# Mixture of experts after an RWKV block on one core: blocks of first choices before blocks of second choices, and one row of results per token

## The reference

```python
x = x + _layernorm(rwkv(_layernorm(x)))    # k, v, r products, a scan over time, output product
x = x + _layernorm(ffn(_layernorm(x)))

# ffn, with E = 8 experts, K = 2 choices, F = 256
probs = softmax(xf @ router_w)
topw, topi = top_k(probs, 2)
routed = sum over the two choices of topw * (silu(xf @ w1[e]) @ w2[e])
shared = silu(gate) * up @ shared_down     # gate, up = halves of xf @ shared_gate_up
shared = sigmoid(xf @ shared_gate_w) * shared
return routed + shared
```

## Time and profile before

| | us |
|---|---|
| median of 3 runs | 1823.32 (1821.41 to 1824.04) |
| the profiled execution | 1822.15 |
| its span, first to last instruction | 1820.0 |
| stage 1, until the first block is loaded | to 1128.82 |
| stage 2, until the results' first load | 1128.82 to 1656.10 |
| stage 3 | 1656.10 to 1820.0 |
| granted TensorE clock, mean | 0.927 of full speed |

### The profile page before, as it was taken

The page is one execution under the profiler, slowest core; times in us unless marked ns, Lnnn a source line. Parts: engine busy times, 40 slices in busy tenths (PEclk is TensorE's granted clock), DMA queues, the critical chain, the costliest instruction groups (busy, mean ns, idle before and its releaser), DMA issues.

```text
span 1820.0 us, 34848 instructions
## 1 busy us (share of the span) xinstructions
PE 1514.6 (83%) x9764; PEld 1345.2 (74%) x9764; DVE 1469.1 (81%) x3533; ACT 1393.5 (77%) x2577; POOL 1074.7 (59%) x985
## 2 busy tenths in 40 slices
PE   4899999999999999999999835999999999980000
PEld 3678888888888888888888734999888888870000
DVE  4799989999998989989898754887776777764888
ACT  3799999999999999999999863776666666651444
POOL 1245545455564645556464441688888888886556
PEclk8999999999999999999999966999999999995555
DMA  5123434343332433333342234898888888877997
GB/s 202 47 89 115 139 116 133 118 148 102 118 128 97 142 106 128 109 116 122 106 142 84 93 108 151 243 189 148 145 145 145 144 144 145 147 114 230 415 417 305
DMA packets 184044, 274.67 MB, mean 151 GB/s; under 512 B 17713, under 2 KB 139569, under 8 KB 183857
## 3 DMA queue, kind: packets, MB, share of 16 engines
q1 hardware_dynamic: 132688, 201.37, 32.6%
q0 software_dynamic: 51168, 71.07, 22.1%
HBM read 127.53 MB, written 144.85 MB: 150 GB/s over the span
## 4 chain that ended last, share of the span: by engine, by line
PE 54%; issue 11%; POOL 11%; DMA 8%; DVE 7%; ACT 3%; DVEq 1%; SPq 1%; ACTq 0%; POOLq 0%
PE PS L1289 42%; POOL d_y L547 8%; PE PS L1281 3%; PE PS L1465 3%; PE PS L1483 2%; POOL d_xd L522 2%; DMA d_y<-x,ixb 2%; PE PS L1352 1%; DMA al<-d_y 1%; DMA shh<-d_y 1%; DMA d_y<-nx,ixb 1%; PE PS L1350 1%; DVE bst L881 1%; PE PS L1443 1%; DVEq L1244 1%
## 5 line engine op out<-in xcount | busy, mean ns | idle before, releaser
L522 POOL DMA_INDIRECT d_xd<-h2n,ixs x256 | 321.2, 1255 | 275.1 <-DVE h2n L1060 194.4
L1289 PE MATMUL PS<-hTh,wqh 128*128 128x512 f32 x768 | 306.5, 399 | 15.8 <-ACT kk L581 10.5
L1289 PE MATMUL PS<-hTh,wql 128*128 128x512 f32 x768 | 306.6, 399 | 0.0
L1289 PE MATMUL PS<-hTl,wqh 128*128 128x512 f32 x768 | 306.2, 399 | 0.0
L1289 PEld LDWEIGHTS PS<-hTh,wqh 128*128 128x128 f32 x768 | 146.4, 191 | 50.7 <-ACT kk L581 11.4
L547 POOL DMA_INDIRECT d_y<-xin,ixb x90 | 141.7, 1575 | 52.6 <-DVE xin L1235 27.0
L1289 PEld LDWEIGHTS PS<-hTh,wql 128*128 128x128 f32 x768 | 146.2, 190 | 34.6
L1289 PEld LDWEIGHTS PS<-hTl,wqh 128*128 128x128 f32 x768 | 146.1, 190 | 33.6
L547 POOL DMA_INDIRECT d_y<-x,ixb x90 | 142.3, 1581 | 27.4 <-issue 20.7
L547 POOL DMA_INDIRECT d_y<-nx,ixb x90 | 141.5, 1572 | 27.4 <-issue 22.6
L482 POOL TENSOR_SCALAR var<-mv 128x4 f32<-128x4 f32 x64 | 62.5, 977 | 148.9 <-DVE mv L886 148.7
(11 more groups left out here) (301 smaller groups left out, 5630.5 us busy)
## 6 DMA issues: line engine op xcount, KB each, us to landing
d_y<-ysh SPq DMA_DIRECT2D x64, 512.0 KB
xin<-in_L_attn_x SPq DMA_DIRECT2D x32, 512.0 KB, 3.9
x<-in_L_attn_x SPq DMA_DIRECT2D x32, 512.0 KB, 3.9
d_x<-x SPq DMA_DIRECT2D x32, 512.0 KB
kk<-d_xd SPq DMA_DIRECT2D x34, 272.0 KB
vv<-d_xd SPq DMA_DIRECT2D x34, 272.0 KB
tr<-d_xd SPq DMA_DIRECT2D x34, 272.0 KB
dl<-d_xd SPq DMA_DIRECT2D x33, 272.0 KB
```

The costliest lines, as they stand in the source:

```text
L522: g.indirect_dma_start(d_xd, bass.IndirectOffsetOnAxis(ap=ixs[:, k:k + 1], axis=0), h2n[:, j, :], None).then_inc(s_sct, 16)
L1289: ins = mm_(out_ap, l, r, start=(k == 0), stop=(k == len(todo) - 1))
```

## The change

- `d_xd` becomes two tensors, one for first choices and one for second. Ranks, positions, counts and tables have a leading axis of 2. Stage 2 has two halves of NB1 = 71 blocks each (64 + 7), NB = 142 in all.
- The shared expert's row is no longer written to `d_y` by SP (64 stores of 512 KB). POOL scatters it (`shared_scatter`, 4 indirect DMAs a chunk) to `d_xs`, at the row that the token's first choice has in its block. In the first half of stage 2 SP loads 256 rows of `d_xs` into `yb` beside each block (`load_shared`), `y_out` adds the expert's result to them, and POOL scatters the sum to `d_y` without adding in DRAM. In the second half the scatter adds in DRAM as before. Between the halves POOL waits for all of its scatters of the first.
- `d_y` has one row per token. Stage 3 loads 512 KB a chunk instead of twice that, and `total` is gone. 14 chunks of x1 instead of 12 are loaded during stage 2.
- The zero blocks: SP writes 8 + 3 before stage 2, ACT writes 8 (for `d_xs`) behind its last `shared_out`, and SP the 8 for second choices between the first loads of stage 2.
- Banks and order in stage 1: `pV[1]` and `pU[0]` move to PS0, `pRK` to PS4; the second `gate_up_product` of `pU` moves ahead of `proj(0, i-1, 0)`; `weighed` moves behind `shared` on DVE; `own_exp` moves to the end of the step before on ACT. `shared_out` of a chunk waits until the rows of the chunk before have been scattered.

```diff
-    NB = 2 * N // BLK + E - 1
+    NF = N // BLK
+    NB1 = NF + E - 1
+    NB = 2 * NB1
...
-        pV = [PS[1], PS[5]]
+        pV = [PS[1], PS[0]]
...
-        pU = [PS[4], PS[3]]
+        pU = [PS[0], PS[3]]
...
-        pRT, pRK = PS[0], PS[0]
+        pRT, pRK = PS[0], PS[4]
...
# SP, stage 1
-                if on(i - 6):
-                    sp.wait_ge(s_ys, n(i - 6, NT, NT))
-                    for s in range(2):
-                        sp.dma_start(ys_a[s, i - 6], ysh[:, :, :]).then_inc(s_st2, 16)
...
+            def tail_2(e):
+                r = sp.value_load(tail[0:1, 1, e:e + 1], min_val=0, max_val=E * CAP - BLK)
+                sp.dma_start(d_xd[1][bass.ds(r, BLK), :].rearrange("(p j) d -> p j d", p=P), zt).then_inc(s_tail2, 16)
...
# SP, before stage 2
+            sp.wait_ge(s_tail, 16 * (2 * E + 3))
+            sp.wait_ge(s_scy, 16 * NT * NCH)
...
+            def load_shared(b):
+                if b >= NYB:
+                    sp.wait_ge(s_yo[b % NYB], 32 * (b // NYB))
+                r = sp.value_load(tabx[0:1, 0, b:b + 1], min_val=0, max_val=E * CAP)
+                sp.dma_start(yb[b % NYB], d_xs[bass.ds(r, BLK), :].rearrange("(p j) d -> p j d", p=P)
+                             ).then_inc(s_yl[b % NYB], 16)
...
             for b in range(NB):
+                if b == NB1:
+                    sp.wait_ge(s_tail2, 16 * E)
                 load_block(b)
+                if 1 <= b <= E:
+                    tail_2(b - 1)
...
+                if 0 <= b - 2 < NB1:
+                    load_shared(b - 2)
                 if b >= 8 and b - 8 < NS:
                     load_rest(b - 8)
...
# POOL
+            def shared_scatter(m):
+                pool.wait_ge(s_pl, n(m, NPL, L_IX))
+                for j in range(NT):
+                    pool.wait_ge(s_ys, n(m, NT, j + 1))
+                    g.indirect_dma_start(d_xs, bass.IndirectOffsetOnAxis(ap=ixs[:, m % 2, j:j + 1], axis=0),
+                                         ysh[:, j, :], None).then_inc(s_scy, 16)
...
-            for i in range(NCH + 4):
+            for i in range(NCH + 6):
...
+                if on(i - 4):
+                    scale_o(i - 4)
+                if on(i - 5):
+                    scatter(i - 5, 0)
+                    scatter(i - 5, 1)
+                if on(i - 4):
+                    scale_h2(i - 4)
                 if 0 < i < NCH:
                     scale_in(i)
+                if on(i - 6):
+                    shared_scatter(i - 6)
...
+                if w < NB1:
+                    for j in range(2):
+                        g.indirect_dma_start(d_y, bass.IndirectOffsetOnAxis(ap=ixb[:, w % 8, j:j + 1], axis=0),
+                                             yb[w % NYB][:, j, :], None).then_inc(s_yo[w % NYB], 16)
+                else:
+                    if w == NB1:
+
+                        for i in range(NYB):
+                            pool.wait_ge(s_yo[i], 32 * ((NB1 - i + NYB - 1) // NYB))
...
# ACT
-                    act.wait_ge(s_st2, 32 * m)
+                    act.wait_ge(s_scy, 16 * NT * m)
...
+            act.wait_ge(s_zt, 2)
+            act.wait_ge(s_tab, 1)
+            for e in range(E):
+                r = act.value_load(tail[0:1, 0, e:e + 1], min_val=0, max_val=E * CAP - BLK)
+                A.dma_start(d_xs[bass.ds(r, BLK), :].rearrange("(p j) d -> p j d", p=P), zt[:, :, 0:D]).then_inc(s_tail, 16)
             A.preload_act_table(ACT.Silu)
...
# DVE, stage 1
-                if on(i - 3):
-                    weighed(i - 3)
                 if on(i - 5):
                     shared(i - 5)
                 if on(i - 3):
+                    weighed(i - 3)
                     sums(i - 3)
...
# DVE, stage 2
+                    if w < NB1:
+                        V.scalar_tensor_tensor(out=t, in0=part, scalar=cwb[:, w % 8, j:j + 1], in1=t, op0=ALU.mult,
+                                               op1=ALU.add).then_inc(s_y, 1)
+                    else:
+                        V.tensor_scalar(t, part, cwb[:, w % 8, j:j + 1], None, ALU.mult).then_inc(s_y, 1)
...
# DVE, stage 3
-                V.tensor_tensor(oC[c % NO], y0C[c % NY], y1C[c % NY], ALU.add).then_inc(s_sum, 1)
...
# PE, stage 1
-                    free((i - 4, s_pl, NPL, L_TB), (i - 4, s_ro, NRO, R_LG), (i - 2, s_k, 2, 2))
+                    free((i - 4, s_mul, 2, 1), (i - 4, s_ro, NRO, R_LG), (i - 2, s_v, 2, 2), (i - 2, s_k, 2, 2))
                     proj(0, i - 1, 1, pK, s_pk)
```

More of the change, by code:

```diff
@@ L52, in rwkv_moe @@
     out_c = out.rearrange("b (c p j) d -> (b c) p (j d)", j=NT, p=P)
-    d_xd = nc.dram_tensor("d_xd", [E * CAP + BLK, XW], F32).ap()
-    NSINK = E + NB - NF + 1
-    d_y = nc.dram_tensor("d_y", [2 * N + 1 + NSINK * BLK, D], F32).ap()
-    ys_a = d_y[1:2 * N + 1, :].rearrange("(s c j p) d -> s c p j d", s=2, j=NT, p=P)
+    d_xd = [nc.dram_tensor(f"d_xd{s}", [E * CAP + BLK, XW], F32).ap() for s in range(2)]
+    d_xs = nc.dram_tensor("d_xs", [E * CAP + BLK, D], F32).ap()
+    NSINK = E + NB1 - NF + 1
+    d_y = nc.dram_tensor("d_y", [N + 1 + NSINK * BLK, D], F32).ap()
     with ExitStack() as ctx:
@@ L275, in rwkv_moe @@
         s_yo = [sem(f"s_yo{i}") for i in range(6)]
+        s_yl = [sem(f"s_yl{i}") for i in range(6)]
         s_Tx = sem("s_Tx")
@@ L286, in rwkv_moe @@
         s_y = sem("s_y")
-        s_cx = [sem(f"s_cx{i}") for i in range(12)]
-        s_cy2 = [sem(f"s_cy2{i}") for i in range(6)]
-        s_sum = sem("s_sum")
+        s_cx = [sem(f"s_cx{i}") for i in range(14)]
         s_nrm = sem("s_nrm")
@@ L386, in _ @@
             sp.dma_start(x1[:, :, :], x_v[0]).then_inc(s_xr, 16)
-            for i in range(NCH + 6):
+            for i in range(NCH + 4):
                 if i % 2 == 0 and i // 2 < E:
@@ L475, in _ @@
             for e in range(E):
-                last = g.memset(tb[:, e:e + 1], float(e * CAP))
+                last = g.memset(tb[:, :, e:e + 1], float(e * CAP))
             last.then_inc(s_const, 1)
@@ L762, in _ @@
             for i in range(NCH + 5):
-                if on(i - 3):
-                    own_exp(i - 3)
                 if on(i - 5):
@@ L807, in _ @@
                     alpha(i - 2)
+                    own_exp(i - 2)
                 if on(i - 3):
@@ L837, in _ @@
                 act.wait_ge(s_nb[3 + c % 2], c // 2 + 1)
-                act.wait_ge(s_sum, c + 1)
+                if c >= NO:
+                    act.wait_ge(s_out[c % NO], 16 * (c // NO))
                 for j in range(NT):
                     at = slice(j * D, (j + 1) * D)
-                    A.activation(oC[c % NO][:, at], oC[c % NO][:, at], ACT.Identity, scale=rstd[:, 3 + c % 2, j:j + 1],
+                    A.activation(oC[c % NO][:, at], yC[c % NY][:, at], ACT.Identity, scale=rstd[:, 3 + c % 2, j:j + 1],
                                  bias=nb[:, 3 + c % 2, j:j + 1]).then_inc(s_nrm, 1)
@@ L1193, in _ @@
             step(4)
-            V.tensor_tensor_scan(cum[:, :], ones8[:, :], nbk[:, :], zero[:, 0:1], ALU.mult, ALU.add).then_inc(s_tb, 1)
-            V.tensor_scalar(wstep[:, :], nbk[:, :], -float(BLK), float(CAP), ALU.mult, ALU.add).then_inc(s_tb, 1)
-            step(6)
-            V.tensor_tensor(big[:, :, :], iotb[:, :].unsqueeze(2).to_broadcast([P, NBP, E]),
-                            cum[:, :].unsqueeze(1).to_broadcast([P, NBP, E]), ALU.is_ge).then_inc(s_tb, 1)
+            for s in range(2):
+                V.tensor_tensor_scan(cum[:, s, :], ones8[:, :], nbk[:, s, :], zero[:, 0:1], ALU.mult, ALU.add).then_inc(s_tb, 1)
@@ L1203, in _ @@
+            step(9)
+            V.tensor_tensor(big[:, :, :, :], big[:, :, :, :], wstep[:, :, :].unsqueeze(2).to_broadcast(over), ALU.mult
                             ).then_inc(s_tb, 1)
-            step(9)
-            V.tensor_reduce(tbf[:, 1, :], big[:, :, :], AX_X, ALU.add).then_inc(s_tb, 1)
             step(10)
-            V.tensor_tensor(tbf[:, 1, :], tbf[:, 1, :], iot2[:, :], ALU.add).then_inc(s_tb, 1)
+            V.tensor_reduce(tbf[:, 1, :, :], big[:, :, :, :], AX_X, ALU.add).then_inc(s_tb, 1)
@@ L1208, in _ @@
             step(11)
+            both = [P, 2, NBP]
+            V.tensor_tensor(tbf[:, 1, :, :], tbf[:, 1, :, :], iot2[:, :].unsqueeze(1).to_broadcast(both), ALU.add
+                            ).then_inc(s_tb, 1)
+            step(12)
             V.tensor_scalar(iot2[:, :], iot2[:, :], -(NF - 1.0) * BLK, None, ALU.add).then_inc(s_tb, 1)
-            step(12)
-            V.scalar_tensor_tensor(out=tabo[:, :], in0=tbf[:, 0, :], scalar=E - 0.5, in1=iot2[:, :], op0=ALU.is_ge,
-                                   op1=ALU.mult).then_inc(s_tab, 1)
@@ L1214, in _ @@
-            V.tensor_scalar(tabx[:, :], tbf[:, 1, :], float(E * CAP), None, ALU.min).then_inc(s_tab, 1)
-            V.tensor_scalar(tabe[:, :], tbf[:, 0, :], float(E - 1), None, ALU.min).then_inc(s_tab, 1)
-            V.tensor_scalar(tabp[:, :], tbf[:, 0, :], float(E - 1), 1024.0, ALU.min, ALU.mult).then_inc(s_tab, 1)
+            step(13)
```

(5 more changed lines are left out.)

218 lines of the change are left out of this document (110 added, 108 removed).

## The result

The changed kernel took 1846.24 us, the median of 4 runs (1842.98 to 1848.57), beside 1823.16 for the kernel before: ratio 1.0124, 95% interval 1.0111 to 1.0137. It is slower by 23 us where 19 us less were forecast, and outside the range. The profiled execution has a span of 1845.5 us (1820.0 before). The same program, run again later on chips 6, 13 and 1, took 1793.5, 1795.8 and 1840.0 us; most of what follows is about that.

The account below looks back on a forecast made before the run. PE was taken to bound stage 1, POOL to set stage 2's end, DMA to bound stage 3. Terms 0 + 15.9 + 2.1 - 36.9 = -18.9 gave 1803.3 us profiled, 1804 as median; range for 8 in 10: 1788 to 1829.

Parts of the forecast that it names:

- so POOL needs 2.5 to 3.1 us a block, and PE's 3.39 decides: 241 us: Stage 2, first 71 blocks: plain scatters at 0.96 us instead of 1.55 leave PE's pitch as the bound.
- Stage 2 otherwise: Stage 2 as a whole: +2 us (-3 to +12), 506 us against 504 before.
- up to 10 us: Stage 2, 14 blocks with an x1 load: DMA at 390 GB/s, near stage 3's 412, may cost up to 10 us.
- The drain: Between stage 2's halves: next scatter about 4.3 us after the last, where 2.1 was the pitch, so +2.2 us.
- Between the stages: Hand-over from stage 1 to 2: +16 us (+10 to +19), as scatters, shared_out and ACT's zero blocks lack cover.
- The low end of +10: Hand-over: if ACT issues a zero block in 0.56 us, the last shared rows decide, landing near 1139: +10 us.
- Stage 3: Stage 3: -37 us (-51 to -24), 3.78 us a chunk with x1 loads and 3.3 without.
- The 0.3 added for POOL: Stage 3, 13 chunks without x1: DVE needs 3.0 us, POOL 3.2 with its gaps; 3.3 us a chunk was taken.
- Stage 1: Stage 1: 0 us (-1 to +5); POOL's extra scatters fit idle time, period stays 31.91 us, scale_o 1.1 us late.
- Plain scatters cost POOL as much as adding ones: Rival in stage 2: plain scatters cost POOL as much as adding ones, +26 us, so 1831 us; chance 0.08.
- The turning point: Stage 2, in that rival: the whole change turns slower when the first half's pitch reaches 3.66 us a block.
- the fourth rival: Stage 3 at its floor, or ACT's zero blocks issued fast at the hand-over: -6 to -14 more, 1790 to 1798 us; chance 0.17.

Follow-up runs that it names:

- the recorded run: The changed kernel's first measured and profiled run, against the kernel before: median 1846.24 us, ratio 1.0124, profiled span 1845.5 us.
- three unrelated edits: Changed kernel, first half of y_out only scaling: 1796.72 us; shared-row loads removed as well: 1789.38; PE's three stage 2 waits for itself removed: 1788.22.

## Why the prediction was wrong

**The step that failed** is stage 2's "so POOL needs 2.5 to 3.1 us a block, and PE's 3.39 decides: 241 us". The first half took 299.4 us, 4.2 a block. The price of the plain scatter was right (0.96 us), POOL had room (73 of 160 us), and PE's own work is no longer than 3.39. What was missing is a term for waits of PE for its own completions, which are told late beside plain scatters. Shown: it appears with plain scatters alone, in the kernel before too; it does not with adding ones on the same chip; PE itself goes on (the burst of three updates); 25 us come back when PE doesn't wait for itself, 20 of them out of the 44 that lateness costs. Not shown: what in the chip does it, why chips 0 and 1 and not 6, 9 and 13, why PE is on time beside the scatters to `d_xd`, and whether it happens when no records are taken. The chip of the recorded run isn't known; its completions are late in the same pattern.

**Could it have been read before?** Not the delay: the kernel before has plain scatters only to `d_xd`, beside which every update of PE is on time. What could be read is the risk: `block_in`, `block_hidden` and `block_out` each wait for work that PE has only just issued, with hardly any slack. The prediction does not name those waits and so puts them at nothing; PE showed 72 of 72 us busy, which hides them.

**Stage 2 otherwise.** On chip 6 the first half took 249.2 us where 243 were forecast, and stage 2 +8.4 where +2.1 were: PE had 57.31 of 60 us while x1 was loaded, with the DMA engines full. That is the "up to 10 us" that the sum put at nothing. The drain was 1400.68 - 1396.01 = 4.7 us (4.3). The second half was 264.8 to 266.8 us (265 by the same measure).

**Between the stages** +7.0 (+4.9 on chip 6) instead of +15.9. The mechanism was right, ACT's zero blocks end last, at 1.22 us each. The mis-sized term is the start: the last eight scatters of `d_xd` begin at 1104.3 and end at 1115.2, not at 1109.9 and 1121.1, so `shared_out` begins at 1122.1 and not at 1128.9. Their start was taken from the kernel before although POOL's order around them changes. (The low end of +10 also leaves out the 1.3 us to the first load that the sum itself has.)

**Stage 3** -42.3 (-41.7) instead of -36.9: 3.76 us a chunk with x1 (3.78 forecast), 2.91 without (3.3). DVE alone had given 3.0, and it decides. The 0.3 added for POOL was wrong: its four operations fit. The Trainium skill's rule on interference (page "SBUF — State Buffer", section "Who interferes with whom") gave 3.0 and -41, and the trace bears it out: POOL's L503 takes 0.25 us at 1729.40, where `final` does not run, and 1.04 where it starts beside `final`, which has two SBUF inputs (1808.93 to 1810.12). L504, the `nmn` of the earlier trace rows, comes behind it and takes 0.23, as no `total` runs beside it any more.

**Stage 1** 0, as forecast: 31.88 us a period, PE 859.61 of 860 us, `scale_o` 0.5 us late (1.1 forecast). Its completions are late there as well, beside `d_xs`, and it costs nothing: with completions on time PE is busy for 860.00 of 860 us. Probably PE's waits have slack there; that was not tested.

**The rivals.** "Plain scatters cost POOL as much as adding ones" had the right sign, the right place and the wrong engine: they cost POOL 0.96 us and PE up to 1 us of waiting a block. The turning point that it named, a first half at 3.66 us a block, was passed. On chips 6 and 13 the time falls into the fourth rival's, "stage 3 falls to its floor, or ACT issues zero blocks fast" (1790 to 1798), partly by luck: stage 3 gained 5 us more than forecast, ACT's zero blocks were not fast, the hand-over was 11 us better because it began earlier, and stage 2 was 6 us worse.

## What to carry to other kernels

An engine's wait for its own last instruction looks free in a profile with the engine busy all the time, and costs when completions are told late. Where the results allow it, take such waits out before making anything around them faster. (Letting one look a block further back was tried only where completions are on time: 3.0 us.) And before an edit is credited with the removal of a loss, run the unedited kernel beside it: here three unrelated edits seemed to cure the same loss, and it was the place where they ran. A verdict of 1% either way for one program (1.0124, 0.9842) can be a matter of where it runs; if the reason is known, the edit that makes the kernel insensitive to it is worth more than the difference.

## What the runs showed of the hardware

- On chips 0 and 1, and in the recorded run, PE's semaphore updates come late beside indirect DMAs without an operation to `d_y` or `d_xs`: beside `d_y` 639 of 761 in the interval from 0.4 to 1.6 us behind the scatter's start, by 0.36 us at the median and by up to 2.2. On chips 6, 9 and 13 it is none of 1220. With adding scatters it is 3 of 726, and those by under 0.1 us.
- In the same traces about a third of the semaphore update records is missing (17,271 in the recorded run, 25,262 on chip 6, for the same 36,132 instructions).
- An indirect DMA of 128 rows of 1 KB takes POOL 0.96 us plain and 1.55 us adding, 0.30 us apart. In the first half of stage 2 the plain one has a median of 1.06 to 1.10 us on chip 6, where DVE is busy 133 of 160 us, and 0.96 in the recorded run, where DVE is busy 114.
- POOL's L503, 128x4, takes 0.25 us where DVE has no instruction with two SBUF inputs, and 1.04 where it starts beside one.
- A second half of plain scatters instead of adding ones is worth 30 us here: 1793.5 against 1763.2, with PE instead of POOL as the bound.
